# Second attention: scores laid out by head from 32x32 pieces, with masked keys in place of masked queries

## The reference

```python
q, k, v = heads(q), heads(k), heads(v)              # 16 heads of 8 features
scores = einsum('bhqd,bhkd->bhqk', q, k) / sqrt(8)
allowed = (j <= i) & (i - j < 64)
attn = softmax(where(allowed, scores, -inf), axis=-1)
ctx = einsum('bhqk,bhkd->bhqd', attn, v)
x = x + ctx @ w_out.T + b_out
```

## Time and profile before

| | us |
|---|---|
| timed runs, lowest / median / highest of 3 | 1000.75 / 1002.17 / 1002.77 |
| span of the profiled execution, first to last instruction | 997.6 |
| median less the span | 4.6 |
| PE busy in the span | 911.7 (91%) |
| POOL / DVE / ACT busy | 661.2 / 647.7 / 611.6 |

### The profile page before, as it was taken

One profiled execution on the slowest core, in us unless ns is written; L12 is line 12 of the kernel. 1 busy time (PEld: TensorE's weight loads), 2 busy tenths in 40 slices (PEclk: granted clock), 3 DMA queues, 4 the chain that ended last, 5 costly groups with the idle time before them and its releaser, 6 DMA issues.

```text
span 997.6 us, 16805 instructions
## 1 busy us (share of the span) xinstructions
PE 911.7 (91%) x5472; PEld 627.0 (63%) x5472; DVE 647.7 (65%) x1447; ACT 611.6 (61%) x1875; POOL 661.2 (66%) x610
## 2 busy tenths in 40 slices
PE   3267899899999999999999999999999998999998
PEld 1144566686666666586666666677666666657665
DVE  5886867688658638697739737787735347437432
ACT  4345566984664575895674575797455377386432
POOL 7676878657688649666759857756765545646554
PEclk8567999989999999999999999999999999999999
DMA  5005252014353524610433534520333560350452
GB/s 185 0 3 135 46 129 72 16 45 108 88 127 87 121 79 96 155 44 12 96 87 88 127 98 85 146 65 18 84 99 81 139 156 12 84 132 12 85 129 63
DMA packets 64762, 85.68 MB, mean 86 GB/s; under 512 B 5218, under 2 KB 30627, under 8 KB 64419
## 3 DMA queue, kind: packets, MB, share of 16 engines
q1 hardware_dynamic: 64674, 84.62, 35.2%
HBM read 79.32 MB, written 5.28 MB: 85 GB/s over the span
## 4 chain that ended last, share of the span: by engine, by line
PE 61%; ACT 11%; POOL 7%; issue 5%; DVE 4%; DVEq 0%; ACTq 0%; POOLq 0%
PE bank L1545 16%; PE bank L1522 8%; PE bank L1524 8%; PE bank L1523 8%; ACT probs L1089 5%; PE bank L1581 4%; PE bank L1566 4%; POOL work L881 3%; PE bank L1595 2%; PE bank L1559 1%; PE bank L1405 1%; POOL kv_terms L846 1%; DVE probsT L1345 1%; PE bank L1399 1%; POOL rstd L833 1%
## 5 line engine op out<-in xcount | busy, mean ns | idle before, releaser
L881 POOL TENSOR_TENSOR work<-work,spread_w 128x512 f32<-128x512 f32 x256 | 336.3, 1325 | 165.4 <-DVE work L1303 162.3
L1303 DVE TENSOR_TENSOR work<-work,bank 128x512 f32<-128x512 f32 x256 | 173.6, 681 | 214.0 <-ACT work L1064 128.1
L1545 PE MATMUL bank<-work,down_w 128*128 128x512 f32 x512 | 263.9, 599 | 9.3 <-POOL work L881 7.4
L1064 ACT ACTIVATE work<-bank 128x512 f32<-128x512 f32 x256 | 151.2, 596 | 182.1 <-PE bank L1524 178.6
L1089 ACT ACTIVATE probs<-bank,neg_max 128x96 f32<-128x96 f32 x512 | 166.0, 382 | 8.2 <-DVE neg_max L1331 5.7
L1522 PE MATMUL bank<-z_hi,gate_hi 128*128 128x512 f32 x256 | 167.0, 652 | 3.6 <-ACT elu L974 2.0
L889 POOL TENSOR_TENSOR probs<-probs,prob_inv 128x768 f32<-128x768 f32 x64 | 94.1, 1470 | 74.0 <-DVE prob_inv L1339 74.0
L1089 ACT ACTIVATION_READ_ACCUMULATOR probs<-bank,neg_max 128x1 f32 x512 | 125.6, 248 | 0.0
L1545 PEld LDWEIGHTS bank<-work,down_w 128*128 128x128 f32 x512 | 94.6, 189 | 40.5 <-POOL work L881 15.0
L1524 PE MATMUL bank<-z_hi,gate_lo 128*128 128x512 f32 x256 | 102.4, 400 | 0.0
L1522 PE MATMUL bank<-z_hi,up_hi 128*128 128x512 f32 x256 | 102.0, 398 | 0.0
(11 more groups left out here) (154 smaller groups left out, 1466.2 us busy)
## 6 DMA issues: line engine op xcount, KB each, us to landing
spread_w<-comb_dram SPq DMA_DIRECT2D x96, 512.0 KB, 6.7
spread_w<-comb_dram SPq DMA_DIRECT2D x128, 128.0 KB, 3.0
vals<-v_dram SPq DMA_DIRECT2D x16, 384.0 KB, 4.1
x_buf<-x SPq DMA_DIRECT2D x8, 256.0 KB, 3.4
v_dram<-v_tok SPq DMA_DIRECT2D x8, 256.0 KB, 4.5
out<-xs SPq DMA_DIRECT2D x8, 256.0 KB, 3.8
spread_w<-wg SPq DMA_DIRECT2D x1, 1024.0 KB, 6.5
spread_w<-wu SPq DMA_DIRECT2D x1, 1024.0 KB, 8.5
```

The costliest lines, as they stand in the source:

```text
L881: pool.tensor_tensor(work[:, n % WORK], work[:, n % WORK], spread_w[:, n // EACH % 2, s % EACH], ALU.mult).then_inc(hid_gated, 1)
L1064: act.activation(work[:, n % WORK], bank[GATE_BANKS[ring_of(row, f, s)]], ACT.Silu).then_inc(silu_ready, 1)
L1303: dve.tensor_tensor(work[:, n % WORK], work[:, n % WORK], bank[UP_BANKS[ring_of(row, f, s)]], ALU.mult).then_inc(gated_ready, 1)
L1545: pe.matmul(bank[Y_BANK], down_w[:, c], work[:, n % WORK], start=(c == 0), stop=(c == CH - 1)).then_inc(down_done, 1)
```

## The change

The rows of a bank are now the 128 queries of the tile (block b, query), its columns (head j, key). The queries are copied once, unmasked, to `queriesT`; the keys are copied four times with the mask of a head, to `head_keys`. A score product takes a weight of 32 features x 32 queries and streams 4 heads x 96 keys = 384 columns into 32 rows of the bank: it uses a 32x32 piece of the array (row group hg, column group b). The window mask is built in the same way: 8 products of 384 columns for a pair of groups where there were 2. `probsT` holds one group in each of its four parts where it held one block, so the first two turns need the first half of `normalise` alone, and a product of `mix` needs a copy of its own group whatever its block: the wait for the last copy of the tile now stands ahead of all 16 products. `mix` reads 4 runs of 32 elements where it read 128 in a row. To make room, `combT` (the expert weights on their way to DRAM) has one buffer where it had two.

```diff
@@ ACT
-                wait(act, combT_sent, 16 * (fg - 1))
-                act.activation(combT[:, fg % 2], side[0:NE, :], ACT.Copy).then_inc(combT_ready, 1)
+                wait(act, combT_sent, 16 * fg)
+                act.activation(combT[:], side[0:NE, :], ACT.Copy).then_inc(combT_ready, 1)
...
             def keys(row, g):
-                copy_side(keysT[:, WIN + GT * g:WIN + GT * (g + 1)], row, "keys", g)
-
-            def queries(row, g):
...
-                side_product(row, "queries", g)
+                side_product(row, "keys", g)
                 for j in range(HG):
-                    a = act.activation(qm[:, g, :, j, :], side.rearrange("p (b q) -> p b q", q=QB),
+                    a = act.activation(head_keys[:, j, WIN + GT * g:WIN + GT * (g + 1)], side,
                                        ACT.Copy, scale=q_mask[:, j:j + 1])
                 a.then_inc(side_taken, 1)
+
+            def queries(row, g):
+                copy_side(queriesT[:, GT * g:GT * (g + 1)], row, "queries", g)
@@ DVE
-            def turned(row, i, blocks):
+            def turned(row, i, pair):
                 wait(dve, mix_ready, tile(row, i))
-                for b in blocks:
-                    dve.wait_ge(probsT_ready, tile(row, i) * NB + b + 1)
-                    dve.tensor_copy(probsT[:, b], bank[4 + b % 2][0:KW, :]).then_inc(probsT_copied, 1)
+                for hg in pair:
+                    dve.wait_ge(probsT_ready, tile(row, i) * HG + hg + 1)
+                    dve.tensor_copy(probsT[:, hg], bank[4 + hg % 2][0:KW, :]).then_inc(probsT_copied, 1)
@@ PE, score
-                    pe.matmul(bank[hg][:, 0:NB * KW], same_query[feats].rearrange("p j q -> p (j q)"),
-                              window[feats, min(i, 1)].rearrange("p b k -> p (b k)"), start=True, stop=False,
-                              tile_position=(QB * hg, 0), skip_group_check=True)
                 for b in range(NB):
-                    first = P * i + QB * b
+                    of_block = slice(QB * b, QB * (b + 1))
                     for hg in pair:
                         feats = slice(QB * hg, QB * (hg + 1))
-                        mm = pe.matmul(bank[hg][:, KW * b:KW * (b + 1)],
-                                       qm[feats, i // T, NB * (i % T) + b].rearrange("p j q -> p (j q)"),
-                                       keysT[feats, first:first + KW], start=False, stop=(b == NB - 1),
-                                       tile_position=(QB * hg, 0), skip_group_check=True)
+                        pe.matmul(bank[hg][of_block, 0:HG * KW].rearrange("p (j k) -> p j k", k=KW), same_query[feats, 0],
+                                  window[feats, min(i, 1), b].unsqueeze(1).broadcast_to([QB, HG, KW]), start=True,
+                                  stop=False, tile_position=(QB * hg, QB * b), skip_group_check=True)
+                for b in range(NB):
+                    of_block, first = slice(QB * b, QB * (b + 1)), P * i + QB * b
+                    for hg in pair:
+                        feats = slice(QB * hg, QB * (hg + 1))
+                        mm = pe.matmul(bank[hg][of_block, 0:HG * KW].rearrange("p (j k) -> p j k", k=KW),
+                                       queriesT[feats, first:first + QB], head_keys[feats, :, first:first + KW],
+                                       start=False, stop=True, tile_position=(QB * hg, QB * b), skip_group_check=True)
@@ PE, turn_probs
-                pe.wait_ge(probs_normed, 2 * (tile(row, i) + 1))
+                pe.wait_ge(probs_normed, 2 * tile(row, i) + pair[0] // 2 + 1)
@@ PE, mix
+                pe.wait_ge(*copied_of(row, i, HG - 1))
                 for b in range(NB):
-                    pe.wait_ge(*copied_of(row, i, b))
                     for hg in range(HG):
                         feats = slice(QB * hg, QB * (hg + 1))
-                        mm = pe.matmul(bank[6][feats, P * b:P * (b + 1)],
+                        mm = pe.matmul(bank[6][feats, P * b:P * (b + 1)].rearrange("p (j q) -> p j q", q=QB),
                                        vals[:, i // 2 % 2, NB * (i % 2) + b, QB * hg:QB * (hg + 1)],
-                                       probsT[:, b, P * hg:P * (hg + 1)], start=True, stop=True,
-                                       tile_position=(0, QB * hg))
+                                       probsT[:, hg].rearrange("p (j q) -> p j q", q=P)[:, :, QB * b:QB * (b + 1)],
+                                       start=True, stop=True, tile_position=(0, QB * hg))
```

More of the change, by code:

```diff
@@ L510, in hybrid_block @@
         top_sum, top_inv = sb("top_sum", [P, T]), sb("top_inv", [P, T])
-        comb, combT = sb("comb", [P, T, NE]), sb("combT", [NE, 2, GT])
+        comb, combT = sb("comb", [P, T, NE]), sb("combT", [NE, GT])
         comb_dram = nc.dram_tensor("comb_dram", (DEEP, NE, GT), F32, kind="Internal").ap()
@@ L517, in hybrid_block @@
         yT = sb("yT", [P, GT])
-        seqT, keysT = sb("seqT", [P, WIN + SEQ]), sb("keysT", [P, WIN + SEQ])
-        qm = sb("qm", [P, G, NB * T, HG, QB])
+        seqT, head_keys = sb("seqT", [P, WIN + SEQ]), sb("head_keys", [P, HG, WIN + SEQ])
+        queriesT = sb("queriesT", [P, SEQ])
         vals = sb("vals", [KW, 2, 2 * NB, D])
@@ L624, in chunk_there, with copied_of @@
             return chunk(row, f, s) - past[0] if past else None
-        def copied_of(row, i, b):
-            return probsT_copied, tile(row, i) * NB + b + 1
+        def copied_of(row, i, hg):
+            return probsT_copied, tile(row, i) * HG + hg + 1
         def run_steps(steps, period, place, at):
@@ L663, in send_weights @@
                     wait(sp, loaded, 32 * (1 + of_parity) * (fg - 2))
-                sp.dma_start(comb_dram[fg % DEEP], combT[:, fg % 2]).then_inc(combT_sent, 16)
+                sp.dma_start(comb_dram[fg % DEEP], combT[:]).then_inc(combT_sent, 16)
                 sp.wait_ge(combT_sent, 16 * (fg + 1))
@@ L1084, in exponentials @@
                 act.wait_ge(max_ready, tile(row, i) * HG + hg + 1)
-                wait(act, probsT_ready, (tile(row, i) - 1) * NB)
+                wait(act, probsT_ready, (tile(row, i) - 1) * HG)
                 wait(act, inv_ready, 2 * (tile(row, i) - 1))
-                for b in range(NB):
-                    m = hg * NB + b
-                    a = act.activation(probs[:, i % 2, m], bank[hg][:, b * KW:(b + 1) * KW], ACT.Exp,
+                for j in range(HG):
+                    m = hg * HG + j
+                    a = act.activation(probs[:, i % 2, m], bank[hg][:, j * KW:(j + 1) * KW], ACT.Exp,
                                        bias=neg_max[:, i % 2, m:m + 1], accum_out=prob_sum[:, i % 2, m:m + 1])
@@ L1330, in maxima @@
                     wait(dve, probs_ready, (tile(row, i) - 2) * HG + hg + 1)
-                    dve.tensor_reduce(neg_max[:, i % 2, hg * NB:(hg + 1) * NB],
-                                      bank[hg][:, 0:NB * KW].rearrange("p (b k) -> p b k", k=KW),
+                    dve.tensor_reduce(neg_max[:, i % 2, hg * HG:(hg + 1) * HG],
+                                      bank[hg][:, 0:HG * KW].rearrange("p (j k) -> p j k", k=KW),
                                       AX_X, ALU.max, negate=True).then_inc(max_ready, 1)
@@ L1518, in gate_up @@
                     elif after is not None:
-                        for b in (NB - 2, NB - 1):
-                            pe.wait_ge(*copied_of(after[0], after[2] - 1, b))
+                        for hg in (HG - 2, HG - 1):
+                            pe.wait_ge(*copied_of(after[0], after[2] - 1, hg))
                     dst = bank[banks[ring_of_chunk]]
@@ L1570, in score, with turn_probs @@
                         if b == NB - 1:
                             mm.then_inc(scores_ready, 1)
-            def turn_probs(row, i, blocks):
-                pe.wait_ge(probs_normed, 2 * (tile(row, i) + 1))
-                for b in blocks:
-                    if b >= 2:
-                        pe.wait_ge(*copied_of(row, i, b - 2))
+            def turn_probs(row, i, pair):
+                pe.wait_ge(probs_normed, 2 * tile(row, i) + pair[0] // 2 + 1)
+                for hg in pair:
+                    if hg >= 2:
+                        pe.wait_ge(*copied_of(row, i, hg - 2))
@@ L1578, in turn_probs @@
                     elif tile(row, i):
-                        pe.wait_ge(*copied_of(0, tile(row, i) - 1, b + 2))
-                    for hg in range(HG):
-                        mm = pe.transpose(bank[4 + b % 2][0:KW, P * hg:P * (hg + 1)],
-                                          probs[:, i % 2, hg * NB + b], ident[:])
+                        pe.wait_ge(*copied_of(0, tile(row, i) - 1, hg + 2))
+                    for j in range(HG):
+                        mm = pe.transpose(bank[4 + hg % 2][0:KW, P * j:P * (j + 1)], probs[:, i % 2, hg * HG + j], ident[:])
```

5 lines of the change are left out of this document (2 added, 3 removed).

## The result

| | before | after |
|---|---|---|
| timed runs, lowest / median / highest of 5 (us) | 1000.12 / 1001.48 / 1002.77 | 1010.73 / 1016.29 / 1021.46 |
| ratio of the runs, with its 95% interval | | 1.0156 [1.012, 1.0192] |
| span of the profiled execution (us) | 997.6 | 1008.9 |
| mean granted clock of that execution | 0.962 | 0.961 |
| mean granted clock of the other timed runs | | 0.951 to 0.955 |

What follows compares the result with a forecast made beforehand. PE was taken as the bound, with DVE and ACT right under it. Rows 1 and 2 4.0, row 3 2.0, row 0 1.0: +7.0 on span 997.6 gives 1004.6, plus 4.6 makes 1009.2 us; range 1002 to 1020.

Steps and rivals of the forecast that it cites:

- The mix's wait closes a loop: Attention tiles: last copy, mix, next turns and DVE's list form a loop of 5.85 us against 5.40, 0.45 more per tile.
- DVE's leg: Loop term: DVE's work from a tile's first copy to the end of its last, without a hole, 4.07 us.
- turns to copy: Loop term: from the start of a pair of turns until DVE can start the first copy, 0.72 us.
- The hand-over from the copy to PE: Loop term: from the end of the last copy to PE's mix, 0.05 us.
- Eight pieces at a time: Scores: 2 row groups by 4 column groups run at once, so a pair takes 0.99 us against 1.13.
- Four at a time: Rival on the scores: row and column groups do not add up, a pair takes 1.81 us, total 1045; chance 0.07.
- halves in order: Rival on the scores: second halves stream before anything behind them starts, a pair takes 3.25 us, total 1138; chance 0.05.
- The 0.14 per pair is not seen: Scores: the 0.14 us saved per pair does not show, since PE then waits some 0.7 us ahead of each mix.
- the gain is kept: Rival on the mix: the last copy is there when PE comes, PE needs 5.12 per tile, 6 us gained, 996; chance 0.07.
- Of 0 to 0.35 us per set I take 0: Masked copies on ACT, eight sets: covered between chunks, so 0; if cover fails, 0.3 us at five places, 1.5 in all.
- The clock had no term in the sum: Granted clock below 1.00 in rows 1 and 2, where PE has holes, was only a sign of being wrong.
- the wait's +1.0: Row 0: one interval is PE-bound and the last mix has no cover, so the wait costs 1.0 us.

Runs made afterwards that it cites:

- e1: The kernel before with one edit: the mix waits for the last copy ahead of its first product; median 1011.0 us, ratio 1.0108.
- e7: The changed kernel with queries and keys exchanged in PLAN, so the four masked copies on ACT come in their old slot; median 1012.2 us, ratio 1.0119.
- e11: The changed kernel with one copy awaited per mix quarter (wrong probabilities), idle filling products at the heads, queries and keys exchanged; median 994.4 us, ratio 0.9931.
- e12: The changed kernel with idle filling products at the heads of parts and queries and keys exchanged; median 1003.3 us, ratio 1.0036.
- e8: The changed kernel with one copy awaited per mix quarter (wrong probabilities) and idle filling products at the heads; median 998.6 us, ratio 1.0012.
- e6: The changed kernel with a tile's first turns ahead of the previous tile's mix and idle filling products at the heads; median 1006.0 us, ratio 1.0057.
- e9: The changed kernel with first turns ahead of the previous tile's mix, idle filling products, and queries and keys exchanged; median 997.2 us, ratio 0.9956.
- e5: The changed kernel with idle f32 products of 512 columns ahead of the second and third tiles' scores; median 1010.8 us, ratio 1.0117.
- e2: The changed kernel with each mix quarter waiting for one copy again (it multiplies wrong probabilities); median 1005.9 us, ratio 1.0062.
- e3: The changed kernel with the first turns of a tile ahead of the mix of the tile before; median 1018.1 us, ratio 1.0176.

## Why the prediction was right and wrong

- **The mix's wait closes a loop: right, its size a little short.** Forecast 5.85 for each tile and some 0.7 of idle ahead of the mix; measured 5.98 and 0.90 to 1.02. Of the loop's terms, DVE's leg was 4.09 (forecast 4.07), the mix 1.01 to 1.03 (1.01), turns to copy 0.74 (0.72). The hand-over from the copy to PE was 0.14 instead of the 0.05 that I took from a row of "issue" in the earlier trace rows, which was not one between these two engines. Over the first five intervals of row 1 the loop cost 2.6 where I had 2.0, and the two parts of row 3 cost 2.7 together where I had 2.0. As a whole the wait is worth 8.9 (e1), against 7.0.
- **Eight pieces at a time: right.** 0.93 for a pair, forecast 0.99, and the 16 products took 0.65 in the chain, as worked out. Four at a time and halves in order are out. In the trace the first halves of a group's eight products start within 23 ns of each other (at 440.38 us) and their second halves 0.32 us later. The rule cited from the Trainium skill (TensorE: Matmul & The Clock Gate, Part 3: Packing small matmuls) would, with adjoining halves, have given 3.25 for a pair; that is not what happened. No trace shows in which order TensorE's list holds the halves, so it stays open whether the rule fails or the halves do not adjoin.
- **"The 0.14 per pair is not seen": nearly right.** e1 has the wait without the new scores and lies at +8.9; the change without the copies' move, e7, at +6.6. The shorter scores thus gave back some 2 us beside the wait. Without the wait they are worth about as much, 2.8 (e11), not the 6 of the rival "the gain is kept": in e11's trace ACT is busy 5.23 of 5.23 us from one mix of row 1 to the next, and PE stands 0.28 for its exponentials. That ACT is the bound there is read, not tested.
- **"Of 0 to 0.35 us per set I take 0": wrong.** This is the first step that failed. The move of the copies measured 4.9 and 5.0 (e7, e12), and 4.0 and 7.3 in the two other pairs (e8 and e11, e6 and e9), where even the bound was 1.5. I asked only whether the next product on PE finds the bank free. That term was right where it applies: four copies take 2.42, a chunk 2.24, and PE stood 0.27; they did not come down towards 0.60 each either (0.69, as before). In row 0 the cover is missing (1.64). What the term left out is ACT's list: what stands behind the copies comes 1.8 us later than in e7, and once, at `yT`, PE waits for just that (1.98 against 0.16). The two kinds of wait make 3.3 of the 4.9; the rest is not traced, and no larger than the scatter of the runs.
- **The clock had no term in the sum: wrong.** This is the second step that failed. The clock was named only under what would make the forecast wrong, and for the holes in front of the mix in rows 1 and 2, which e1 and e5 have at full clock. It fell at the heads of the parts, where PE is sooner through with its scores and stands in front of the exponentials. Row 3's first part is less clear: there the clock fell behind the second hole in front of a mix in the change and in e5, and at the end of it in e1 with the old scores; e12 has the same hole (1.31) at full clock. The clock is worth 4.1 us by the change's median; filling the heads brought 5.5 (change to e5), 7.3 (e2 to e8) and 12.1 (e3 to e6). Nor does one measurement tell 2 us from no change, as the prediction had it: the 71 of the kernel before on record and the one at 0.914 go from 993.1 to 1007.3.
- **Together:** wait 8.9, copies 4.9, shorter scores -2.3 (worked out as what is missing to 11.5), clock 4.1: 15.6 against 14.8 measured. The scores' part is worked out from the rest, so that the sum comes near is no proof of it. The forecast had 7.0, all of it for the first.
- **Open:** the number of stretches at half clock differs from run to run of one kernel, and why a head falls in one run and not in another can't be told from these runs. The column at equal clock assumes that lost clock costs every kernel the same as the kernel before. Row 0 came out 2.4 shorter up to its last mix, where I had +1.0. It had less half clock up to there (61 us against 72 in the kernel before), which the line would price at 3.0 us, so the wait's +1.0 may be in it; with the wait alone (e1) that mix came 3.1 later, with 78 us of half clock. No experiment took row 0 apart.

## What to carry to other kernels

When a layout changes which axis a buffer is split on, look at each consumer's waits: four waits of a quarter each hid copies that landed 0.5 to 0.6 us after the start of the mix, and one wait for all put them on the path, whatever the shorter products gave. A step that is moved is priced on every engine's list that it passes, not by the one buffer that it fills. And before a difference of one per cent is explained, set the runs against each other at the same mean granted clock: here runs of one kernel differed by 12 us along with the clock, two edits that did shorten the loop (e2, e3) looked like failures, and e9 looked like a winner.

## What the runs showed of the hardware

Eight f32 products on 32x32 pieces (two row groups by four column groups) ran at once: 16 instructions of 384 columns in 0.65 us, where one takes 0.325 on the whole array.

TensorE's granted clock fell to its lower level (1.2 of 2.4 GHz) at the head of row 2's part, after windows of 5 us in which PE had been busy 3.75 and 4.53 and had not stood still longer than 1.42 at a time. Four idle products of 512 columns per part kept it at 1.00 there, and the kernel was faster for doing more; in one part of 28 they did not. How busy PE is does not by itself tell where the clock falls: the kernel before kept 1.00 in row 3 through windows of 3.68 and 3.85 of 5 (832 to 842 us).

The hand-over from the end of a DVE copy to the start of the product that waits for it was 0.14 us, at both mixes of the tile shown (438.05 and 444.03).
